# Transposing attention probabilities in 32x32 blocks on VectorE with a round trip through DRAM, and a new order of steps, in a macaron block on one core

## What is computed

```python
x = L0_attn_x                                     # (8, 512, 256), float32
x = x + 0.5 * ffn_ref(layernorm(x), wqkv, ...)    # two local layers
x = x + attn_ref(layernorm(x), weight)            # global attention, 16 heads of 16
x = x + 0.5 * ffn_ref(layernorm(x), wqkv, ...)    # two local layers again

def layer(x, ...):                                # one local layer, run twice in ffn_ref
    h = shift_token(x)
    q, k, v = split(h @ wqkv)                     # 8 heads of 64
    q, k = rotary_xpos(l2norm(q) * qs, l2norm(k) * ks)
    # windows of 128 tokens; each query window sees its own and the previous window, causal
    p = softmax(mask(8 * q @ k.T))                # einsum bhwid,bhwjd->bhwij
    x = x + (p @ v) @ wo
    h = layernorm(shift_token(x)) * g + b
    a, g = split(h @ w1 + b1)
    return x + (a * gelu(g)) @ w2 + b2
```

## Time and profile before

| | |
|---|---|
| median of 3 runs | 3908.85 us (3904.86 to 3909.45) |
| profiled execution, its own time | 3903.55 us |
| its span, first to last instruction | 3901.9 us |
| PE busy over the span | 3688.1 us (95%) |
| DVE busy | 2631.9 us (67%) |
| ACT busy | 2132.6 us (55%) |
| POOL busy | 2147.3 us (55%) |
| DMA, mean | 41 GB/s |

### The profile page before, as it was taken

One profiled execution on the slowest core, in us unless ns is written; L12 is line 12 of the kernel. 1 busy time (PEld: TensorE's weight loads), 2 busy tenths in 40 slices (PEclk: granted clock), 3 DMA queues, 4 the chain that ended last, 5 costly groups with the idle time before them and its releaser, 6 DMA issues.

```text
span 3901.9 us, 74698 instructions
## 1 busy us (share of the span) xinstructions
PE 3688.1 (95%) x23040; PEld 3005.1 (77%) x23040; DVE 2631.9 (67%) x7110; ACT 2132.6 (55%) x5040; POOL 2147.3 (55%) x2179
## 2 busy tenths in 40 slices
PE   3999999999999799999999999999999999999997
PEld 2777777777777678888888888877777777777776
DVE  6777777777777555565555655666777777777774
ACT  2665675566655444444444444446566755666564
...
DMA packets 245007, 160.82 MB, mean 41 GB/s; under 512 B 122748, under 2 KB 225800, under 8 KB 244744
## 3 DMA queue, kind: packets, MB, share of 16 engines
...
## 4 chain that ended last, share of the span: by engine, by line
PE 83%; DVE 7%; issue 4%; POOL 3%; ACT 2%; DMA 1%; DVEq 0%; SPq 0%; ACTq 0%; POOLq 0%
PE psum L1395 21%; PE psum L1396 20%; PE psum L1397 20%; PE psum L1509 6%; PE psum L1519 5%; PE psum L1539 4%; PE psum L1498 3%; PE psum L1624 3%; POOL ge_lo L741 1%; DVE probs L1103 1%; PE psum L1475 1%; DVE turned_sin L1069 1%; DVE nT_lo L1165 1%; DVE ssq L1076 1%; POOL rinv L684 1%
## 5 line engine op out<-in xcount | busy, mean ns | idle before, releaser
L741 POOL TENSOR_TENSOR ge_lo<-ge,ge_hi 128x512 fp32r<-128x512 f32 x512 | 672.6, 1316 | 530.4 <-PE psum L1397 288.6
L923 ACT ACTIVATE ge<-psum 128x512 f32<-128x512 f32 x512 | 306.4, 598 | 669.3 <-PE psum L1624 669.2
L702 POOL TENSOR_SCALAR probs<-probs,rz 128x256 f32<-128x256 f32 (+1 forms) x1024 | 446.1, 456 | 358.7 <-DVE rz L1117 358.7
L1289 DVE CAST ge_hi<-ge 128x512 fp32r<-128x512 f32 x512 | 265.9, 522 | 497.5 <-ACT ge L923 497.4
L847 ACT ACTIVATE probs<-probs,nb,rq 128x256 f32<-128x256 f32 (+1 forms) x1024 | 574.9, 564 | 21.9 <-DVE nb L1111 18.8
L1103 DVE CUSTOM_DVE_ANT_0 probs<-psum,mask 128x256 f32<-128x256 f32 (+1 forms) x1024 | 339.3, 387 | 256.0 <-PE psum L1509 199.7
L684 POOL TENSOR_TENSOR rinv<-ssq,minus_half 128x16 f32<-128x16 f32 x124 | 376.1, 3034 | 127.7 <-DVE ssq L1080 124.2
L714 POOL TENSOR_TENSOR hid_lo<-gate,hid_hi 128x512 fp32r<-128x512 f32 x160 | 206.5, 1290 | 324.6 <-ACT hid_hi L879 324.6
L1395 PE MATMUL psum<-wqkv_hi,hT_hi 128*128 128x512 f32 x768 | 318.3, 414 | 5.9 <-DVE hT_lo L1054 3.4
L828 ACT ACTIVATE squares<-psum 128x512 f32<-128x512 f32 x256 | 153.2, 599 | 286.9 <-PE psum L1397 269.0
L1395 PE MATMUL psum<-nT_hi,w_hi 128*128 128x512 f32 x704 | 296.6, 421 | 11.3 <-DVE gate L1177 6.0
...
## 6 DMA issues: line engine op xcount, KB each, us to landing
xnext<-stream SPq DMA_DIRECT2D x32, 512.0 KB, 4.2
xmid<-stream SPq DMA_DIRECT2D x32, 512.0 KB, 3.8
gaT<-y_turned SPq DMA_DIRECT2D x256, 64.0 KB, 2.0
y_turned<-probs SPq DMA_DIRECT2D x192, 64.0 KB, 2.9
stream<-xmid SPq DMA_DIRECT2D x16, 512.0 KB, 2.9
wo_hi<-y_turned SPq DMA_DIRECT2D x128, 64.0 KB, 2.0
wo_lo<-y_turned SPq DMA_DIRECT2D x128, 64.0 KB, 2.0
...
```

The source lines that it names most:

```text
L702: last = nc.gpsimd.tensor_scalar(pu, pu, rz[:, h, t:t + 1], 1.0, ALU.mult, ALU.mult)
L741: nc.gpsimd.tensor_tensor(ges[1][:, k % 4, :], ge[:, k % 4, :], f32(ges[0][:, k % 4, :]), ALU.subtract).then_inc(S["g_lo"], 1)
L923: nc.scalar.activation(ge[:, k % 4, :], RB[k % 2], ACT.Exp, scale=GSCALE, accum_out=gz[:, h, t:t + 1]).then_inc(S["g_exp"], 1)
L1289: V.tensor_copy(ges[0][:, k % 4, :], ge[:, k % 4, :]).then_inc(S["g_hi"], 1)
```

## The change

The probabilities of a unit are no longer transposed on PE. Three things take the place of `T`, `H` and `L`:

1. `V` on DVE: one transpose instruction (two for the unit of 6 blocks) which turns each 32x32 block in itself, from `probs` to a new tile `p_blocks`.
2. `st` on SP: one DMA that stores the unit (384 or 512 KB) to a DRAM tensor `p_turned`. `ld` on SP: four DMAs of 32 partitions each that load it to `pT`, so that each 32x32 block lands where the whole transpose would have it.
3. `A` reads `pT` through an access pattern with pieces of 32 columns.

Beside this, the scores of odd units go to the banks TB0 and TB1, which are free now (`SCORES`); `c` moves from DVE to POOL; SP gets a list of its own (`SP_STEPS`); and all lists have a new order. In the new order the token transposes `n` and all of `g`, `a` and `w` carry a `-`: the feed-forward part of a sequence now runs wholly in the next round.

```diff
-PE_STEPS = ("S0 -a2 -g3 S1 -w0 -g4 S2 -a3 -w1 S3 T0 -w2 T1 -a4 S4 T2 A0 S5 A1 A2 S6 T3 -w3 S7 T4 A3 -w4 +z0 +z1 "
...
+PE_STEPS = ("-n0 -n1 v3 Q2 -g0 Q3 K2 S0 -g1 K3 -a0 S1 -a1 S2 S3 -a2 -g2 S4 S5 -w0 -w1 S6 -g3 S7 A0 A1 +z0 +z1 "
+            "-w2 -a3 +q0 A2 A3 +k0 -a4 -g4 -w3 +k1 -g5 A4 A5 +q1 -w4 -w5 +k2 A6 A7 W0 W1 +q2 W2 W3 +K0 B +v0 "
...
+ACT_STEPS = ("-G1 Kc3 E0 -u0 E1 E2 i0 -u1 E3 i2 -G2 E4 i1 -u2 E5 O0 +zh0 +zh1 -G3 E6 -u3 O1 +sk0 +sq0 E7 -G4 "
...
+DVE_STEPS = ("-j1 ss3 -nl0 -nl1 rk3 Y X0 -y0 X1 R0 -y1 X2 i0 V0 R1 X3 R2 V1 X4 i2 R3 V2 -y2 X5 i1 V3 R4 X6 R5 "
+            "P0 +zl0 +zl1 V4 -y3 X7 V5 R6 P1 +rk0 +rq0 R7 V6 -y4 V7 -y5 +ss0 +rq1 -F -e +rk1 +ss1 P2 P3 +ss2 x "
+            "B f0 +rk2 +rq2 l r f1 +rq3 j0 f2").split()
...
+SP_STEPS = ("-old wq wo wf0 st0 st1 ld0 +xin st2 ld1 st3 ld2 ld3 st4 st5 ld4 wf1 ld5 st6 st7 ld6 ld7 -keep res "
+            "shift wf2").split()
...
+POOL_STEPS = ("b3 p3 d3 c3 N0 -ul0 N1 -ul1 N2 N3 -ul2 N4 N5 -ul3 N6 +d0 N7 -ul4 +b0 -ul5 +b1 +p0 +c0 +p1 +d1 +p2 "
...
+    p_turned = nc.dram_tensor("p_turned", (4, P, 8 * P), F32, kind="Internal").ap()
...
-    pT = sb("pT", [P, 2, 2, 4 * P], c=ffn_mem)
+    pT = sb("pT", [P, 14 * P], c=ffn_mem)
...
+    p_blocks = sb("p_blocks", [P, 14 * P], c=ffn_mem)
...
+    SCORES = [RB, TB]
...
+        def p_keep(m, i):
+
+            w, turn_ = unit_blocks(i) * P, UNITS // 2 * m + i // 2
+            need_apart(sp, (S["dve_v"], UNITS * m + i + 1), (S[f"p_in{i % 2}"], 16 * P // SQ * (turn_ - 1)))
+            sp.dma_start(p_turned[i % 4, :, 0:w], p_blocks[:, unit_columns(i)]).then_inc(S[f"p_kept{i % 2}"], 16)
+
+        def p_rows(m, i):
+
+            w, turn_ = unit_blocks(i) * P, UNITS // 2 * m + i // 2
+            need_apart(sp, (S[f"p_kept{i % 2}"], 16 * (turn_ + 1)), (S["pe_av"], UNITS * m + i - 1))
+            q = P // SQ
+            for k in range(q):
+                sp.dma_start(pT[k * SQ:(k + 1) * SQ, unit_columns(i)].rearrange("c (q x) -> c q x", q=q),
+                             p_turned[i % 4, :, k * w // q:(k + 1) * w // q].rearrange("(q c) x -> c q x", q=q)
+                             ).then_inc(S[f"p_in{i % 2}"], 16)
...
+                if kind == "c":
+
+                    pool.wait_ge(S["pool_k"], NT * m + i + 1)
+                    pool.wait_ge(S["pool_r"], NT * m + i + 1)
+                    kv = m1[1][i % 2].rearrange("p (h d) -> p h d", h=HEADS)
+                    nc.gpsimd.tensor_tensor(kv, kv, rinv[:, i, HEADS:2 * HEADS].unsqueeze(2).to_broadcast([P, HEADS, DH]),
+                                            ALU.mult).then_inc(S["pool_c"], 1)
...
-                    copy(pT[:, i % 2, 0, 0:w], TB[0][:, 0:w]).then_inc(S["act_p"], 1)
...
-                            waits.append((S["pe_p"], 2 * (UNITS * m + i - 2)))
+                            waits.append((S["dve_v"], UNITS * m + i - 2))
...
-                    V.tensor_copy(pT[:, i % 2, 1, 0:w], TB[1][:, 0:w]).then_inc(S["dve_p"], 1)
+                if kind == "V":
+                    blocks = unit_blocks(i)
+                    turned = p_blocks[:, unit_columns(i)].rearrange("p (k j r) -> p j k r", k=P // SQ, r=SQ)
+                    kept = probs[:, i % 3].rearrange("p a c -> p (a c)")
+                    need_apart(dve, (S["pool_n"], UNITS * m + i + 1), (S[f"p_kept{i % 2}"], 16 * (UNITS // 2 * m + i // 2)))
+                    for js in [slice(0, blocks)] if blocks == 8 else [slice(0, blocks // 2), slice(blocks // 2, blocks)]:
+                        first = (8 - blocks) // 2 * (1 + 2 * js.start // blocks) + js.start
+                        last = V.transpose(turned[:, js], kept[:, first * P:(first + js.stop - js.start) * P].rearrange(
+                            "p (j k c) -> p j k c", k=P // SQ, c=SQ))
+                    last.then_inc(S["dve_v"], 1)
...
-                        last = turn(TB[side][:, col * P:(col + 1) * P],
-                                    probs[:, i % 3, 2 * side + t - blocks[0], a:a + P], ident[:])
-                        last.then_inc(S["pe_p"], 1)
...
+                    pe.wait_ge(S[f"p_in{i % 2}"], 16 * P // SQ * (UNITS // 2 * m + i // 2 + 1))
+                    rows = pT[:, unit_columns(i)].rearrange("p (q j r) -> p j q r", q=P // SQ, r=SQ)
...
+                            last = mm(summed.rearrange("p (j q r) -> p j q r", q=P // SQ, r=SQ),
+                                      vs[:, j, h * DH:(h + 1) * DH], rows[:, j0:j0 + len(at)],
```

More of the change, by code:

```diff
@@ L27 @@
 LAYERS = 2
+SQ = 32
 ROUNDS = LAYERS * B
@@ L323, in left @@
     def left(table, begun, load):
-        return [t for t in table if load != LAYERS or t not in " ".join(begun.values()).split()]
+        front = "z q k v Q K zh sq sk vh Qc Kc zl rq rk ss Y b d p c".split()
+        done = " ".join(begun.values()).split() + [t for t in table if t.rstrip("0123456789") in front]
+        return [t for t in table if load != LAYERS or t not in done]
     def stage_end(eng, k):
@@ L904, in a_round @@
                            prepared(left(ACT_STEPS, BEGUN_ACT, load), PREP_ACT, call, nxt))
+                if load is not None:
+                    act.wait_ge(S["bias_ok"], load + 1)
             def last(m, final, call=call):
@@ L1263, in a_round @@
                 some_steps(n, prev, nxt, None, load, switch, final, layer,
-                           table=prepared(left(DVE_STEPS, {**BEGUN_DVE, **HEAD_DVE}, load), PREP_DVE, call, nxt))
+                           table=prepared(left(DVE_STEPS, BEGUN_DVE, load), PREP_DVE, call, nxt))
             def last(m, final, call=call):
@@ L1382, in bank_before @@
             behind = ahead + turns - line[at][2]
+            if first_n == ROUNDS and n is not None and n + behind == ROUNDS and k in "zqkvQK":
+                continue
             if n is None or first_n <= n + behind <= last_n:
@@ L1478, in some_steps @@
                     w = "qkv".index(kind)
-                    if fresh_qkv is not None:
+                    if fresh_qkv is not None and m == n + 1:
                         weights_done(pe, w_base(fresh_qkv) + KD)
@@ L1656, in sequence @@
                             pe.wait_ge(S["g_exp"], G_STEPS * B)
[L1657 removed]
+                            if BEGUN_PE[k] == "S1":
+                                read("v", 3, ROUNDS, 0)
+                            some_steps(ROUNDS, False, True, 1, table=BEGUN_PE[k].split(), ahead=True)
                 pe.wait_ge(S["g_zero"], 1)
```

134 lines of the change are left out of this document (58 added, 76 removed).

## The result

The changed kernel took 4034.7 us as the median of 4 runs (4025.4 to 4035.5), the kernel before 3908.0 (3904.9 to 3909.5). The ratio is 1.032, with a 95% interval of 1.0302 to 1.0338. The prediction was 3721 us with a range to 3815, so it is 314 us off and has the wrong sign. The mean granted TensorE clock fell from 0.987 to 0.951.

What follows compares the result with a forecast made beforehand. PE, busy 75.5 of 77.20 us a round, was taken as the bound. Layer 0 saves 5.9 and layer 1 6.6 us in 15 intervals each, 188, 182 after first rounds: 3903.55 - 182 = 3721 us, range 3655 to 3815.

Steps and rivals of the forecast that it cites:

- PE's work: On PE, per round: removing 56 transposes saves 7.4 us, taking 77.2 to 69.8 us.
- rival 4: No change: product A at twice its time on PE gives back 7 of 7.4 us; 3890 to 3905; chance 0.05.
- The small costs: On POOL c takes 1.3 us, bound 3.03; on DVE a block transpose takes 1.24 us for 1024 columns.
- The ring: Chain of waits across engines from one n0 to the next: 9.2 + 32.3 + 17.6 + 9.9 = 69.0 us.
- A0 and A1 stand as near: Detour through DRAM: loads for A0 and A1 are covered about as narrowly as A7's, 7.1 us inside 7.6.
- the slack of A6 and A7: Detour through DRAM: PE's work leaves 6.8 us for A6, 7.6 for A7; A7 has its data after 7.1.
- part (b) of the ring: ACT from E0 to G4: exponentials 18.0, table loads 7.7, thirteen others 6.6, together 32.3 us.
- all crossings: About ten handoffs between engines, 0.1 to 0.2 us each, added as 1.5 us to give 71.3 a round.
- The rival of exposed loads: A unit's four loads don't overlap, A7's data 3.3 to 12.1 us late; slower, up to 4070 us; chance 0.07.
- (d): DVE and the shift from x to j0: 11.3 us before, 9.9 without one sum of squares.
- I let them save the same: Intervals with weight loads stay longer by the same splits as before and save the same as the other intervals.
- 6 us for the first rounds: In the first round of each of two calls nothing covers the detour, costing about 3 us each.

Runs made afterwards that it cites:

- the version of the three orders without the detour: The changed kernel with the input's load first, feed-forward weights' loads last, POOL's power last, and the store and loads left out: 3816.3 us, ratio 0.977.
- the last run above: The changed kernel with the next input's load issued from ACT's queue, behind a wait until unit 1's store has landed: 4055.5 us, ratio 1.038.

## Why the prediction was wrong, step by step

**PE's work: right in size.** 69.8 us were predicted for a round, which is a period and holds the 1.7 us for which PE was idle before. By busy time alone, PE had 75.5 us and has 68.9 in the version of the three orders without the detour, at a clock of 1.00. That is 6.6 less, the lower end of the 6.6 to 7.4 that I had. In the changed kernel it is 70.4 at a clock of 0.98. A reads its pieces of 32 columns at 0.87 us for eight matmuls, against 0.80 or somewhat more before, and over all 2560 of them the mean is 343 ns against 326 before, at the lower mean clock. So rival 4 is out.

**The small costs: right.** c takes 1.04 us on POOL, where 1.3 was taken and 3.03 was the bound, and the transposes take these times on DVE:

```profile
3110.94 1.02 DVE L1164 STREAM_TRANSPOSE p_blocks<-probs 128x384 f32<-128x384 f32 x2
3114.33 1.25 DVE L1164 STREAM_TRANSPOSE p_blocks<-probs 128x1024 f32<-128x1024 f32 x1 [0.16 <-issue]
```

**The ring.** In the round at 3094 its parts are 9.7 us from n0 to E0 (9.2 predicted), 39.4 from E0 to G4's end (32.3), 17.8 from g5 to W3 (17.6) and 11.3 from x to j0 (9.9). Together they are 78.2 of the 78.7 us of the round, so the ring does close. With the queue in order and no detour the steady interval of layer 0 is 72.1 against 71.3. So the ring is a sound model of a round, if its steps keep their lengths. Two did not.

**First failed step: "A0 and A1 stand as near".** I worked out the slack of A6 and A7 and gave A0 and A1 the same in half a sentence. From V1's end (3115.6) to the moment at which PE is ready for A1 (3122.8) it is 7.2 us, and ld1 landed 11.3 us after V1, where the sum had 7.1. I had priced the transfers one at a time. The store took its 2.9 us. Then 1.4 us passed until ld1's first issue, which I had at nothing. From there to the last landing it is 6.9 us instead of 4.2, since `xin` and `st2`, 896 KB, move at the same time: ld1's last load landed after 5.36 us, against 3.58 without `xin`. With `xin` out of the way the two terms are 0.6 and 5.0, so A1 still waits 1.51: even then the price was too low. I asked what SP's queue holds behind ld6 and ld7 and not what it holds ahead of ld1. A6 and A7, which I had worked out, don't wait in this round. ACT stands ahead of O0, which needs A0 and A1 (3.30 us idle there), and this is nearly half of what part (b) of the ring is over: 39.4 instead of 32.3 us. Waits of 0.3 to 0.9 us for DVE's and PE's steps are 2.5 more, where I had added 1.5 us for all crossings. Moving that one load was worth 98 us. The rival of exposed loads had the sign, but another mechanism: it had four loads of a unit going one after the other, which they don't.

**Second failed step: (d), j0 at 2.11 us from the earlier trace rows.** About half of that number was itself a wait. j0 had one whole addition of POOL beside it before, and needs 1.1 us alone, as j1 in the next row of the same group. I moved three operations of POOL beside it and kept the duration. It became 3.8, and n0 waited 2.13 us. Reordering POOL was worth 37 us.

**Third: the edges, "I let them save the same" and 6 us for the first rounds.** They cost 107 us more than before in the profile (51.8 + 54.7), where the sum had them gaining some 56. The detour is 82 of them, by the run without it; the weights' loads in its middle explain 13 to 15 (3900.1 - 3887.1, 3936.7 - 3921.2). In the first rounds nothing hides the transfers; these windows of the changed kernel show a granted clock of 0.57 and 0.60, not far from the lower of its two levels (1.2 GHz of 2.4), while the DMA engines are busy for 69 and 76% of the time. The kernel before had 1.00 and 0.95 there.

```profile
80.00:100.00 20.00, 9.98 (x67) 7.10 (x68) 13.36 (x59) 12.16 (x40) 10.71 (x16) 0.83 0.12 46
100.00:120.00 20.00, 15.16 (x74) 9.49 (x70) 11.74 (x39) 8.63 (x27) 6.51 (x16) 0.57 0.69 210
120.00:140.00 20.00, 10.10 (x36) 6.39 (x37) 9.34 (x17) 4.33 (x12) 6.03 (x8) 0.60 0.76 202
```

**A term that the sum put at nothing: the granted clock.** The rows had 1.00 in a steady round, and I kept that for the new kernel. The clock has two levels, 1.0 and 0.5 of full speed, so a mean over a span gives the time at the lower one (an estimate): 101 us in the kernel before (0.987 over 3902 us), 395 in the changed kernel (0.951 over 4033), 299 with the input's load first (0.962 over 3930), and 214 with the three orders and no detour (0.972 over 3813). A stretch at half the clock can cost PE half of its length, so against the kernel before the lower clock costs the changed kernel at most 147 us, and the version without the detour at most 56. These windows (columns as in the earlier trace rows) begin at A1's start behind its wait, of 4.15 us in the changed kernel, 1.51 with the input's load first, and 2.10 with that load in ACT's queue:

```profile
3127.00:3137.00 10.00, 10.00 (x66) 8.21 (x67) 6.45 (x16) 8.02 (x16) 0.57 (x2) 0.83 0.41 122
3546.50:3556.50 10.00, 9.96 (x73) 8.00 (x74) 7.20 (x19) 9.08 (x21) 4.16 (x9) 1.00 0.51 161
3101.50:3111.50 10.00, 9.96 (x66) 8.17 (x67) 6.52 (x17) 7.99 (x18) 2.57 (x7) 0.83 0.47 150
```

The clock was 0.83 behind the first and the third. So a wait on PE can cost more than its length, and its removal can give back more: with the input's load first the waits at A fell by 64 us in all (136.9 to 72.8) and the time by 98. Not each wait does it. In the last run above PE stood 3.63 us at A1, and the clock was 1.00 in the 10 us behind it.

**The whole way** from 4034.7 to the prediction of 3721, by medians: 98 the input's load beside ld1, 37 j0 beside POOL, 13 the weights' loads, 71 the rest of the detour. These steps hold what each gave back in clock as well. That leaves 95 at 3816, with no detour and all in order, of which the clock is at most the 56 above. There, by the starts of the power, the 20 steady intervals save 98 us of some 125 predicted (five of them, those of layer 1 in the second call, are 2.2 us longer than the same in the first); the ten others save 14 of 62, and start, middle and end cost 23 us (27 + 48 + 23, less the 6 that were priced, is 92). Why these edges don't profit even then I did not test. The trace shows where PE stands: four times 9 us for `w_lo`, 36.2 in all, and once 7.0 and twice 6.2 for DVE's maximum, none of which the kernel before has. The new order also ends a call with all of n, g, a and w of its last sequence, which may be part of it. Also open is how the 71 us split between the clock and the waits.
